# Level 1's loop of a two-level style convolution: the composite convolution by parity as three half-length products

## The reference, cut to what matters

```python
def _layer(x, style, w, b, mw, mb, typ):
    s = style @ mw.T + mb
    weight = SCALE * w * s[:, None, :, None]
    demod = lax.rsqrt(jnp.sum(weight * weight, axis=(2, 3)) + EPS)
    weight = weight * demod[:, :, None, None]
    ...
# TYPES = ('same', 'upsample', 'same', 'downsample'), the kernel size is 3, the blur is (1, 3, 3, 1) / 8
# L1_ffn: W[i, o] = scales[o] * q[i, o] - zeros[o], out = x + conv(x) @ W + bias
```

## Time and profile before

| what | value |
|---|---|
| median of 3 runs | 907.77 us (907.46 to 908.02) |
| profiled execution, its own time | 907.6 us |
| its span from first to last instruction | 906.1 us |
| busy: TensorE / VectorE / ScalarE / GpSimd | 898.8 / 531.7 / 459.8 / 89.6 us |
| instructions on TensorE / VectorE / ScalarE / GpSimd | 5174 / 1248 / 881 / 113 |
| mean granted TensorE clock | 1.000 |

### The profile page before, as it was taken

How to read it: one execution, slowest core, us unless ns; L and a number is a source line. 1 busy time by engine, 2 the same in 40 slices (tenths; PEclk the granted TensorE clock), 3 DMA queues, 4 the chain that set the end, 5 groups by cost and what they waited for, 6 DMA issues and landing times.

```text
span 906.1 us, 15387 instructions
## 1 busy us (share of the span) xinstructions
PE 898.8 (99%) x5174; PEld 825.7 (91%) x5174; DVE 531.7 (59%) x1248; ACT 459.8 (51%) x881; POOL 89.6 (10%) x113
## 2 busy tenths in 40 slices
PE   9999999999999999999999999999999999999998
PEld 8889899899899899899899898888999999999998
DVE  8886445455455455365465465576755566665555
ACT  5955435435445455355355245477455656555540
POOL 0000000000000000000000020302111211111221
PEclk9999999999999999999999999999999999999999
DMA  8701101201201101101102112341222221222111
GB/s 293 247 3 69 69 23 46 69 23 46 69 16 53 50 25 64 46 23 69 46 23 69 62 53 70 65 167 44 93 84 81 93 69 69 69 93 83 57 71 70
DMA packets 33133, 64.30 MB, mean 71 GB/s; under 512 B 11728, under 2 KB 14032, under 8 KB 33104
## 3 DMA queue, kind: packets, MB, share of 16 engines
q1 hardware_dynamic: 24032, 30.90, 11.2%
q0 software_dynamic: 9072, 33.03, 9.7%
HBM read 47.14 MB, written 16.78 MB: 71 GB/s over the span
## 4 chain that ended last, share of the span: by engine, by line
PE 96%; DVE 2%; ACT 2%; issue 0%; ACTq 0%; DVEq 0%
PE conv_ps L184 8%; PE conv_ps L185 8%; PE conv_ps L186 8%; PE fold_ps L728 6%; PE prod_ps L1024 6%; PE prod_ps L1022 6%; PE prod_ps L1023 6%; PE prod_ps L989 5%; PE prod_ps L991 5%; PE prod_ps L990 5%; PE prod_ps L1098 4%; PE prod_ps L1097 4%; PE fold_ps L693 4%; PE turn_ps L943 3%; PE turn_ps L991 2%; PE turn_ps L990 2%
## 5 line engine op out<-in xcount | busy, mean ns | idle before, releaser
L1022 PE MATMUL prod_ps<-b_hi,xt 128*128 128x512 f32 x240 | 93.6, 390 | 0.0
L1024 PE MATMUL prod_ps<-b_hi,xt 128*128 128x512 f32 x240 | 93.5, 390 | 0.0
L1023 PE MATMUL prod_ps<-b_lo,xt 128*128 128x512 f32 x240 | 93.5, 389 | 0.0
L949 ACT ACTIVATE xt<-turn_ps 128x512 fp32r<-128x512 f32 x32 | 17.4, 594 | 136.9 <-PE turn_ps L943 136.9
L989 PE MATMUL prod_ps<-a_hi,xt 128*128 128x384 f32 x240 | 81.2, 338 | 0.0
L991 PE MATMUL prod_ps<-a_hi,xt 128*128 128x384 f32 x240 | 81.1, 338 | 0.0
L990 PE MATMUL prod_ps<-a_lo,xt 128*128 128x384 f32 x240 | 81.1, 338 | 0.0
L1097 PE MATMUL prod_ps<-quant,xt_hi 128*128 128x342 f32 x256 | 80.8, 320 | 0.0
L1098 PE MATMUL prod_ps<-quant,xt_lo 128*128 128x342 f32 x256 | 80.7, 320 | 0.0
L184 PE MATMUL conv_ps<-h_hi,e_hi 128*128 128x512 f32 (+1 forms) x204 | 75.5, 370 | 1.1 <-DVE h_lo L170 1.1
L1082 DVE SCALAR_TENSOR_TENSOR res<-prod_ps,norm,res 128x512 f32<-128x512 f32 x32 | 23.9, 751 | 87.8 <-PE prod_ps L1024 86.7
(11 more groups left out here) (313 smaller groups left out, 2404.0 us busy)
## 6 DMA issues: line engine op xcount, KB each, us to landing
x_in<-in_x SPq DMA_DIRECT2D x64, 128.0 KB, 2.7
res<-in_x POOLq DMA_DIRECT2D x16, 512.0 KB, 3.6
x_after_first<-res POOLq DMA_DIRECT2D x16, 512.0 KB, 2.9
x_in<-x_after_first SPq DMA_DIRECT2D x64, 128.0 KB, 2.7
res<-x_after_first POOLq DMA_DIRECT2D x16, 512.0 KB, 3.5
out_x<-res POOLq DMA_DIRECT2D x15, 512.0 KB, 3.0
a_raw<-in_adapter_in SPq DMA_DIRECT2D x8, 544.0 KB, 8.7
b_raw<-in_adapter_out SPq DMA_DIRECT2D x8, 512.0 KB, 6.9
```

Of the source, the lines that this page charges most:

```text
L1022: nc.tensor.matmul(prod_ps[n][:, :], bufs.xt_hi[:, k, :], bufs.b_hi[:, k, cols], start=(k == 0), stop=False)
L1023: nc.tensor.matmul(prod_ps[n][:, :], bufs.xt_hi[:, k, :], bufs.b_lo[:, k, cols], start=False, stop=False)
L1024: last = nc.tensor.matmul(prod_ps[n][:, :], bufs.xt_lo[:, k, :], bufs.b_hi[:, k, cols], start=False, stop=(k == KT - 1))
```

## The change

In the 12 steps of level 1's loop the composite convolution is done in the second way. `data` and `whole` of level 1 are new buffers of their own (`data1`, `whole1`), shared by all three slots; the sums and the right stream use level 0's. The constant borders of `data1` and one block of `whole1` are cleared once, ahead of the edge copies (three clears for each of the two samples, one for `whole1`), so that the per-pair clears and one copy of `act_fold2_whole` fall away in level 1. The semaphores' counts are shifted by the number of pairs done in the first way (`plain_samples`).

Fold 3, fold 2 and the copy of the whole filter of pair c + 1 are done in the step of pair c; `fold_start` is done for pair c + 2. The step ahead of the loop does folds 3 and 2 of pair 20 between its thirds. In a step TensorE's order becomes: transposes of pair i, layer 1 (a = 0, 1), fold 3 of c + 1, first and second third, fold 2 of c + 1, last third, `pe_three` for a = 0 and 1. The residual of VectorE is cut in two: thirds 0 and 1, and the last third with the final addition, which stands between the two joins. `left` is the number of written-out steps that still follow (3 inside the loop).

```diff
@@ -652,10 +652,12 @@
+DATA_PADS = 2 * (NPAIR - 3) + 2
+    b.plain_samples = (4, 14)[L]
...
@@ -840,13 +843,13 @@
-    v.wait_ge(S.data_pads, 2 * c + a - 3)
+    v.wait_ge(S.data_pads, DATA_PADS if bufs.first_sample else 2 * c + a + 1 - bufs.plain_samples)
...
@@ -865,8 +868,10 @@
-    nc.scalar.activation(flat(whole[C:P, 0:E_PAIRS - 1, :, C:P]), blocks[0:C, 2:2 * E_PAIRS, :], ACT.Identity)
-    nc.scalar.activation(whole[C:P, E_PAIRS - 1, :, C:P], bufs.e_hi[C:P, E_PAIRS - 1, :, C:P].bitcast(F32), ACT.Identity).then_inc(S.fold2_hi, 1)
+    last = nc.scalar.activation(flat(whole[C:P, 0:E_PAIRS - 1, :, C:P]), blocks[0:C, 2:2 * E_PAIRS, :], ACT.Identity)
+    if not bufs.first_sample:
+        last = nc.scalar.activation(whole[C:P, E_PAIRS - 1, :, C:P], bufs.e_hi[C:P, E_PAIRS - 1, :, C:P].bitcast(F32), ACT.Identity)
+    last.then_inc(S.fold2_hi, 1)
 def dve_filter_sums(v, c, bufs):
...
@@ -890,7 +895,9 @@
-def pe_three(pe, c, a, bufs):
+def pe_three(pe, c, a, bufs, ahead=False):
+    if a == 1 and ahead:
+        pe.wait_ge(S.fold2_hi, 2 * c + 3)
...
@@ -903,7 +910,7 @@
 def act_middle(act, c, a, bufs):
-    act.wait_ge(S.middle_done, 2 * c + a - 3)
+    act.wait_ge(S.middle_done, 2 * c + a + 1 - bufs.plain_samples)
...
@@ -1098,13 +1105,15 @@
+def dve_second_residual(v, f, bufs, apart=False, last=False, parts=(0, 1, 2)):
-    for n, cols in enumerate(thirds):
+    if 0 in parts:
+    for n in parts:
...
@@ -1118,7 +1127,7 @@
-    if not last:
+    if not last and 2 in parts:
...
@@ -1187,6 +1196,10 @@
+data1, whole1 = [T1(f"data1{a}", [P, DATA]) for a in range(2)], T1("whole1", [P, E_PAIRS + 2, 2, P])
+for b in buf1:
+    b.data, b.whole = data1, whole1
+    b.sum_hi, b.sum_lo, b.right_hi, b.right_lo = buf0.sum_hi, buf0.sum_lo, buf0.right_hi, buf0.right_lo
 def act_chunks(act, first, end, loaded, raw, hi, ready):
...
@@ -1506,25 +1519,31 @@
     pe_cond(pe, c, 1, slot(c))
     pe.wait_ge(S.quant_ready, KT)
     pe.wait_ge(S.ones_ready, 1)
-    for n in range(3):
-        pe_quant(pe, i, n, slot(i))
-
-    def second_step(i, bufs, after=None):
+    pe_quant(pe, i, 0, slot(i))
+    pe_fold3(pe, c + 1, slot(c + 1))
+    pe_quant(pe, i, 1, slot(i))
+    pe_fold2(pe, c + 1, slot(c + 1))
+    pe_quant(pe, i, 2, slot(i))
+
+    def second_step(i, bufs, left=AHEAD, after=None):
         c = i + AHEAD
-        pe_layer1(pe, c, 0, bufs)
         pe.wait_ge(S.x1_ready, evicted(i))
         pe_turn(pe, i, bufs, True)
-        pe_layer1(pe, c, 1, bufs)
-        pe_fold3(pe, c, bufs)
-        pe_quant(pe, i, 0, bufs)
-        pe_fold2(pe, c, bufs)
-        pe_quant(pe, i, 1, bufs)
+        for a in range(2):
+            pe_layer1(pe, c, a, bufs)
+        if left:
+            pe.wait_ge(S.middle_scaled, 2 * c)
+            pe_fold3(pe, c + 1, bufs)
+        for n in range(2):
+            pe_quant(pe, i, n, bufs)
+        if left:
+            pe_fold2(pe, c + 1, bufs)
         pe_quant(pe, i, 2, bufs)
-        pe_cond(pe, c, 0, bufs)
+        pe_three(pe, c, 0, bufs, left > 0)
         if after:
             pe.wait_ge(S.x1_ready, evicted(i, 3))
             pe_turn(pe, i + 1, after, True)
-        pe_cond(pe, c, 1, bufs)
+        pe_three(pe, c, 1, bufs, left > 0)
     loops = (END - FIRST - 1 - AHEAD) // SLOTS
     with pe.Fori(0, loops - 1) as n:
...
@@ -1716,27 +1735,40 @@
             act_ends(act, f, a, slot(f))
     act_turn(act, NPAIR, slot(NPAIR))
     act.wait_ge(S.turned, 2 * NPAIR + 2)
-    for a in range(2):
-        act_cond(act, c, a, slot(c))
-        act_ends(act, c, a, slot(c))
+    act_cond(act, c, 0, slot(c))
+    act_ends(act, c, 0, slot(c))
+    act_fold_start(act, c + 1, slot(c + 1))
+    act_cond(act, c, 1, slot(c))
+    act_ends(act, c, 1, slot(c))
     split(c + 1, slot(c + 1))
-    act_fold_start(act, c + 1, slot(c + 1))
-
-    def second_step(i, bufs, last=False):
+    act_fold3(act, c + 1, slot(c + 1))
+    act.wait_ge(S.data_pads, DATA_PADS)
+    act_fold2_whole(act, c + 1, slot(c + 1))
+    act_fold_start(act, c + 2, slot(c + 2))
+    act.sem_inc(S.middle_scaled, 10)
+
+    def second_step(i, bufs, left=AHEAD):
         c = i + AHEAD
         act_turn(act, i, bufs)
-        act_layer1(act, c, 0, bufs)
-        act_fold3(act, c, bufs)
-        act_layer1(act, c, 1, bufs)
-        act_fold2(act, c, bufs)
-        if not last:
+        act_filters(act, c, bufs)
+        act_layer1_parity(act, c, 0, bufs)
+        if left:
+            act_fold3(act, c + 1, bufs)
+        act_layer1_parity(act, c, 1, bufs)
+        for a in range(2):
+            act_parity_hi(act, c, a, bufs)
+        if left:
             split(c + 1, bufs)
-            act_fold_start(act, c + 1, bufs)
+            act_fold2_whole(act, c + 1, bufs)
+        if left > 1:
+            act_fold_start(act, c + 2, bufs)
+        act_middle(act, c, 0, bufs)
+        if not left:
+            act_turn(act, i + 1, slot(i + 1))
+        act_middle(act, c, 1, bufs)
         for a in range(2):
-            act_cond(act, c, a, bufs)
+            act.wait_ge(S.cond_out, 2 * c + a + 1)
             act_ends(act, c, a, bufs)
-            if last and a == 0:
-                act_turn(act, i + 1, slot(i + 1))
     loops = (END - FIRST - 1 - AHEAD) // SLOTS
     with act.Fori(0, loops - 1) as n:
...
@@ -1913,6 +1945,9 @@
+    nc.vector.memset(whole1[C:P, E_PAIRS - 1, :, C:P], 0.0)
+    for a in range(2):
+        dve_data_pads(v, c, a, slot(c))
...
@@ -1940,24 +1975,34 @@
     v.wait_ge(S.consts_loaded, 16 * 3)
     f = FIRST
     dve_turn(v, f, slot(f))
+    dve_fold_start(v, c + 1, slot(c + 1))
     split(c + 1, slot(c + 1))
-    dve_fold_start(v, c + 1, slot(c + 1))
+    dve_fold3(v, c + 1, slot(c + 1))
     dve_second_residual(v, f, slot(f))
-
-    def second_step(i, bufs, last=False):
-
+    dve_filter_sums(v, c + 1, slot(c + 1))
+    dve_fold_start(v, c + 2, slot(c + 2))
+
+    def second_step(i, bufs, left=AHEAD):
         c = i + AHEAD
         dve_turn(v, i, bufs)
-        dve_fold3(v, c, bufs)
-        dve_layer1(v, c, 0, bufs)
-        dve_layer1(v, c, 1, bufs)
-        dve_fold2(v, c, bufs)
-        if not last:
+        dve_filters(v, c, bufs)
+        dve_differences(v, c, 0, bufs)
+        if left:
+            dve_fold3(v, c + 1, bufs)
+        dve_differences(v, c, 1, bufs)
+        for a in range(2):
+            dve_parity_lo(v, c, a, bufs)
+        dve_second_residual(v, i, bufs, parts=(0, 1))
+        if left:
+            dve_filter_sums(v, c + 1, bufs)
             split(c + 1, bufs)
-            dve_fold_start(v, c + 1, bufs)
-        dve_second_residual(v, i, bufs)
-        if last:
+        dve_join(v, c, 0, bufs)
+        dve_second_residual(v, i, bufs, parts=(2,))
+        if not left:
             dve_turn(v, i + 1, slot(i + 1))
+        dve_join(v, c, 1, bufs)
+        if left > 1:
+            dve_fold_start(v, c + 2, bufs)
     loops = (END - FIRST - 1 - AHEAD) // SLOTS
     with v.Fori(0, loops - 1) as n:
```

More of the change, by code:

```diff
@@ L825, in dve_data_pads @@
             data = bufs.data[a]
-            v.wait_ge(S.layer1_done, 2 * c + a + 1)
+            if not bufs.first_sample:
+                v.wait_ge(S.layer1_done, 2 * c + a + 1)
             nc.vector.memset(data[:, EVEN:EVEN + SPAN + 1:SPAN], 0.0)
@@ L848, in act_parity_hi @@
         def act_parity_hi(act, c, a, bufs):
-            act.wait_ge(S.differences, 2 * c + a - 3)
+            act.wait_ge(S.differences, 2 * c + a + 1 - bufs.plain_samples)
             data = bufs.data[a]
@@ L1099, in pe_quant @@
             last.then_inc(S.out_done, 1)
-        def dve_second_residual(v, f, bufs, apart=False, last=False):
+        def dve_second_residual(v, f, bufs, apart=False, last=False, parts=(0, 1, 2)):
             g = f - NPAIR
             thirds = [slice(max(n * QCOLS, ONES) - ONES, (n + 1) * QCOLS - ONES) for n in range(3)]
-            v.wait_ge(S.biased, g + 1)
-            v.wait_ge(S.out_done, evicted(f))
-            nc.vector.tensor_scalar(bufs.neg_sum[:, :], hidden_ps[0][:, 0:1], -1.0, None, ALU.mult).then_inc(S.rowsum_read, 1)
-            for n, cols in enumerate(thirds):
+            if 0 in parts:
+                v.wait_ge(S.biased, g + 1)
+                v.wait_ge(S.out_done, evicted(f))
+                nc.vector.tensor_scalar(bufs.neg_sum[:, :], hidden_ps[0][:, 0:1], -1.0, None, ALU.mult).then_inc(S.rowsum_read, 1)
+            for n in parts:
+                cols = thirds[n]
                 ps = conv_ps[0] if apart and n == 2 else hidden_ps[n]
@@ L1534, in _ @@
                 f = FIRST + 1 + SLOTS * (loops - 1) + j
-                second_step(f, slot(f), slot(f + 1) if j == SLOTS - 1 else None)
+                second_step(f, slot(f), SLOTS - 1 - j, slot(f + 1) if j == SLOTS - 1 else None)
             f = END - AHEAD
@@ L1746, in _ @@
                 f = FIRST + 1 + SLOTS * (loops - 1) + j
-                second_step(f, slot(f), last=(j == SLOTS - 1))
+                second_step(f, slot(f), SLOTS - 1 - j)
             for f in range(END - AHEAD + 1, END):
```

## The result

The changed kernel takes 897.13 us (median of 4 runs, 896.68 to 897.48) against 907.88 us for the one before on the same chip (907.46 to 908.02): a ratio of 0.9882, 95% interval 0.9865 to 0.9899. It is faster, by 10.7 us where 13.0 were forecast. The profiled execution took 897.48 us, its span is 895.7, the mean granted clock 0.999.

What follows compares the result with a forecast made beforehand. TensorE, busy for 99% of the span, was taken as the bound. 15.6 - 0.83 - 1.69 - 0.1 = 13.0 us less gave a forecast median of 894.8 us, range 892.9 to 899.5.

Steps and rivals of the forecast that it cites:

- The product: Three half-length products replace the composite convolution in each loop step: 4.32 for 5.62 us, saving 1.30 per step.
- The rival of loads that are not hidden: Twelve more weight loads per step not hidden behind half-length matmuls: 27.4 us in all, 922.2 us, chance 0.02.
- The moved folds and transposes: Folds 3 and 2 run one step earlier, transposes ahead of layer 1; only moved on TensorE, whose step is 18.50 us.
- The ring: ScalarE's and VectorE's chain of work in a loop step: 17.94 us, fitting TensorE's 18.50 with 0.56 to spare.
- B: Rival: the loop's ScalarE and VectorE chain is longer than laid out; 895 to 902.5 us, likeliest near 898, chance 0.14.
- D: Rival: slower, costlier hand-overs in the loop's ScalarE and VectorE chain; 915.1 us with 0.15 more at each, chance 0.04.
- C: Rival: neither the wait before the loop nor the one in the last step costs anything; 892.3 us, chance 0.05.
- both breaks: TensorE's transposes wait for the last third's scaling: 0.83 us before the loop, 1.69 in the last step, once each.
- Does the cover hold?: Walk through a loop step's waits: others finish in time for TensorE; fold 3's low parts at about 8.2, needed at 9.88.
- First wait: Before the loop the transposes wait until the last third is scaled: 0.83 us, once.
- Last wait: In the last step the next pair's transposes wait for join and scaling without cover: 1.69 us, once.
- Clears: Seven clears on VectorE ahead of the loop: about 0.1 us reaches TensorE, ends 0 and 0.5.

Runs made afterwards that it cites:

- e10: e8 with GpSimd's bias addition also waiting for the semaphore that `v_lo` raises: 895.62 us, ratio 0.9862.
- e8: e1 with GpSimd's bias addition for the pair two ahead put behind the finished output's store instead of ahead of it: 908.0 us.
- e2: The changed kernel with the last third scaled and the residual added ahead of the first join, in the last loop step only: 897.55 us.
- e3: The changed kernel with TensorE doing the last third before fold 2 of pair 20, ahead of the loop: 898.24 us.
- e1: The changed kernel with GpSimd adding the bias for the pair two ahead once a pair's output is ready, ahead of its store: 898.9 us.
- e5: The changed kernel with 16 matmuls less per loop step on TensorE and the bias added to 8 columns only: 885.49 us.
- e11: e10 together with e2, e3 and the clears on GpSimd: 893.41 us, ratio 0.9837.
- e7: The changed kernel with e1, e2, e3 and the clears on GpSimd: 896.11 us, ratio 0.9869.

## Why the prediction was right, and where it was short

- **The product** (4.32 for 5.62 us per step): right. 4.30 measured, 0.120 us per matmul, and the weight loads stay hidden. The rival of loads that are not hidden has nothing for it. The sentence of the Trainium skill that the forecast weighed (TensorE: Matmul & The Clock Gate, section on the mechanism, what overlaps) does not hold for these loads: by the page's price a step would be an estimated 1.28 us longer than the 18.49 measured.
- **The moved folds and transposes cost nothing** on TensorE: right. Transposes, layer 1, fold 3 and last third are the row's values; the sum of a step, 18.50, is 18.49 in the kernel without bias and in e10.
- **The ring** (17.94): fits, as said, and is at most 17.57, so it was laid out too long by 0.37 us or more. Rivals B and D fall, and C with them, since both breaks cost what follows.
- **Does the cover hold?** This is the step that failed. It took each VectorE instruction at the duration of a row in which it stood alone, and GpSimd was looked at for its queue (stores and reloads), not for what its 2.40 us do to VectorE. The forecast had fold 3's low parts ready at about 8.2 for 9.88; undisturbed they end at 8.29 (e10), in the step of the changed kernel shown above at 9.99. Price: 14.3 us expected of the eleven steps (11 x 1.30) less 12.56 measured (217.79 less 848.95 - 643.72) = 1.74 us, and about 0.3 in the last step. Leaving the addition out gives back 2.0.
- **First wait** (0.83): 0.70 of waiting, and with the restart, in which eight transposes take 0.99 instead of 0.89, about 0.96 with what stands ahead. The restart's 0.1 lies in the first step and so in the 1.74 as well.
- **Last wait** (1.69): 1.80, and 0.2 more as transposes and the next group start slowly. Without the hold it is 1.5 + 0.2, so the size was right and the excess is the same missed term.
- **Clears** (0.1): seven rows from 598.64 to 599.25, 0.64 us with their gap, and the products beside them took 0.21 us longer. Twice the 0.1 taken, inside its ends of 0 and 0.5.
- Sum: 13.0 - 1.74 - 0.3 - 0.13 + 0.1 (the restart, counted twice) - 0.1 - 0.4 (in this profile everything is 0.42 us later at the first transposes of all, 33.06 against 32.64, long before the change) = 10.4 us; the spans differ by 906.1 - 895.7 = 10.4.

The range held, but partly by luck: its upper part was there for a longer ring, and what used it was something else.

The Trainium skill (SBUF — State Buffer, section on who interferes with whom) states the missed term: a VectorE instruction with two inputs in SBUF contends with a GpSimd instruction that reads SBUF, one with a single SBUF input, outside the two-port modes, does not, and the other side is fully blocked. The traces agree on which are held (`sum_lo`, `e_lo`, `v_lo`, the differences: up to 2.7 us; `xt_lo`: 1.29 as alone) and on how hard. The page also says who wins: whoever issues first has the ports for the whole instruction. These traces neither confirm nor refute that, since by their recorded starts both sides win (see the last section).

## What to carry to other kernels

Before an order is changed, list on one time axis the instructions of VectorE with two SBUF inputs and those of GpSimd that compute, and see which will now stand side by side; here the place of 2.4 us of work on a 10% busy engine decided between nothing (e10) and 12 us (e8). Where there is a free place, pin GpSimd's instruction to it by a semaphore rather than by counting on its start. And a cover is only tested when VectorE is on time: e2 and e3 were worth about three times as much once it was.

## What was not expected of the hardware

- Either side can be the one that waits, and the recorded starts do not tell which. In the step shown at the top `sum_lo` started 0.26 us ahead of the addition and was held, and the addition took its usual 2.40. In the next step it started 0.20 us ahead and took 0.69; here the addition took 2.74, so it was GpSimd that waited, and the next VectorE instruction with two SBUF inputs was held in turn:

```profile
686.39 0.69 DVE L170 TENSOR_TENSOR sum_lo<-whole,sum_hi 128x512 fp32r<-128x512 f32 x1
687.24 2.38 DVE L848 TENSOR_TENSOR data<-data 128x257 f32<-128x257 f32 x1 [0.17 <-ACT data L839]
...
686.59 2.74 POOL L1358 TENSOR_TENSOR res<-res,bias 128x1024 f32<-128x1024 f32 x1
```

The changed kernel has this three times in its ten steps, each time with a step of 18.50 or 18.51. In e3 `sum_lo` starts 0.22 us ahead in two steps; in one it is held (3.17 us), in the other the addition is (2.72). The spans on GpSimd are rough in this profile, so which side asked first stays open.

- The clock. In the profiles of e1, e3, e5, e8 and e11 TensorE's granted clock is 0.66 in a stretch of the edge columns ahead of the loop, where it is 1.00 in the others. The mean of 0.66 means part of the stretch at the lower of its two levels, 1.2 GHz. The stretch of the changed kernel (columns as above):

```profile
626.00:631.00 5.00, 5.00 (x26) 4.25 (x27) 2.53 (x5) 2.57 (x10) 4.60 (x2) 1.00 0.01 2
```

and the same of e1:

```profile
626.00:631.00 5.00, 5.00 (x18) 3.93 (x19) 1.67 (x4) 1.04 (x7) 4.54 (x2) 0.66 0.01 2
```

18 matmuls instead of 26 in the same 5 us: about 1.5 us, and the medians above scatter by that. TensorE had been a little less busy just before it (3.17 of 4.00 us against 3.44), but e7, with 3.16, kept its clock, so what decides stays open. It also means that e11's profiled run holds these 1.5 us, and that differences under 1.5 us between medians were not used here without the steps of the traces.
